# Attention inside a fused block: the transposes of the last query block move ahead of the scores of the third and fourth blocks

## The reference, cut to what matters

```python
q, k, v = (qkv[:, :, 0], qkv[:, :, 1], qkv[:, :, 2])
q = rotary_embedding(q, seq_len, HEAD_DIM)
k = rotary_embedding(k, seq_len, HEAD_DIM)
scores = jnp.einsum('bqhd,bkhd->bhqk', q, k) * scale
mask = jnp.tril(jnp.ones((seq_len, seq_len), dtype=bool))[None, None, :, :]
scores = jnp.where(mask, scores, NEG_INF)
weights = jax.nn.softmax(scores, axis=-1)
out = jnp.einsum('bhqk,bkhd->bqhd', weights, v)
out = out.reshape(batch, seq_len, NUM_HEADS * HEAD_DIM)
return jnp.einsum('bsf,fe->bse', out, W_out)
```

## Time and profile before

| | |
|---|---|
| median of 3 runs | 1304.67 us (1304.54 to 1305.31) |
| the profiled execution: its time | 1303.55 us |
| its span, first to last instruction | 1301.8 us |
| attention loop, first scores to last projection | from about 276 to about 1029 us |
| busy over the span: TensorE / VectorE / ScalarE / GpSimd | 93% / 71% / 59% / 64% |

### The profile page before, as it was taken

How to read it: one execution, slowest core, us unless ns; L and a number is a source line. 1 busy time by engine, 2 the same in 40 slices (tenths; PEclk the granted TensorE clock), 3 DMA queues, 4 the chain that set the end, 5 groups by cost and what they waited for, 6 DMA issues and landing times. The chain is left out here.

```text
span 1301.8 us, 26919 instructions
## 1 busy us (share of the span) xinstructions
PE 1209.9 (93%) x8118; PEld 894.6 (69%) x8118; DVE 929.6 (71%) x2027; ACT 764.2 (59%) x2179; POOL 827.6 (64%) x906
## 2 busy tenths in 40 slices
PE   7799999969999999999999999999999759999992
PEld 5588888846666666666666666666665658888882
DVE  6665344358888888888888888888888677633543
ACT  5655665646666656666656656656565426555552
POOL 4323356158888788787787787676666336766662
PEclk8899999989999999999999999999999959999996
DMA  9151122122221222212221222211221231113223
GB/s 306 38 205 44 49 57 69 39 67 51 60 56 37 57 58 52 52 45 52 59 54 44 51 54 50 49 39 45 50 49 34 90 114 42 47 48 111 61 64 107
DMA packets 86008, 86.44 MB, mean 66 GB/s; under 512 B 11040, under 2 KB 78496, under 8 KB 85104
## 3 DMA queue, kind: packets, MB, share of 16 engines
q1 hardware_dynamic: 74896, 65.50, 18.6%
q0 software_dynamic: 8864, 18.17, 5.2%
q10 hardware_dynamic: 2112, 1.05, 0.3%
HBM read 33.43 MB, written 17.69 MB: 39 GB/s over the span
## 5 line engine op out<-in xcount | busy, mean ns | idle before, releaser
L1605 POOL TENSOR_SCALAR at_prob<-at_prob,at_rec 128x128 f32<-128x128 f32 (+3 forms) x256 | 316.0, 1239 | 162.4 <-DVE at_rec L1787 160.9
L1888 ACT ACTIVATE at_prob<-at_s,at_nb 128x128 f32<-128x128 f32 (+3 forms) x512 | 265.4, 526 | 49.7 <-DVE at_nb L1779 45.2
L960 POOL DMA_INDIRECT f_xb<-xn_dram,f_source x142 | 141.8, 999 | 168.6 <-PE f_b L1007 104.3
L1899 ACT ACTIVATE at_probT<-at_pt 128x128 f32<-128x128 f32 (+3 forms) x256 | 105.0, 436 | 231.1 <-PE at_pt L1711 231.1
L1779 DVE TENSOR_REDUCE at_nb<-at_s 128x2 f32<-128x256 f32 (+3 forms) x256 | 208.6, 816 | 10.9 <-PE at_s L1697 10.9
L1169 DVE TENSOR_TENSOR f_hid<-f_b,f_silu 128x512 f32<-128x512 f32 x142 | 98.5, 693 | 140.5 <-PE f_b L1020 98.7
L1711 PE MATMUL at_pt<-ident,at_prob 128*128 128x128 f32 x1280 | 183.5, 275 | 1.9 <-DVE at_prob L1790 1.2
L1692 PE MATMUL at_s<-at_KT,at_QT 64*128 64x128 f32 (+3 forms) x1024 | 176.1, 463 | 6.1 <-DMA at_KT<-at_probT 4.6
L1773 DVE TENSOR_TENSOR at_turned<-at_pj,rope 128x1024 f32<-128x1024 f32 x122 | 148.8, 1220 | 40.6 <-PE at_pj L1658 40.6
L1723 PE MATMUL at_o<-at_probT,at_V 128*64 128x512 f32 (+3 forms) x1024 | 152.0, 437 | 16.1 <-DVE at_probT L1801 16.1
L1599 POOL TENSOR_TENSOR at_R<-at_turned 128x512 f32<-128x512 f32 x126 | 157.2, 1267 | 2.2 <-DMA at_KT<-at_probT 2.2
(11 more groups left out here) (298 smaller groups left out, 2141.9 us busy)
## 6 DMA issues: line engine op xcount, KB each, us to landing
at_QT<-at_R SPq DMA_DIRECT2D x128, 128.0 KB, 2.3
at_KT<-at_R SPq DMA_DIRECT2D x124, 128.0 KB, 2.3
ys_dram<-y SPq DMA_DIRECT2D x71, 64.0 KB, 1.8
xn_dram<-f_xn SPq DMA_DIRECT2D x16, 256.0 KB, 2.7
f_down<-down_t SPq DMA_DIRECT2D x2, 2048.0 KB, 8.2
f_xb<-xn_dram,f_source POOLq DMA_INDIRECT x142, 2.6
X<-x SPq DMA_DIRECT2D x4, 512.0 KB, 6.2
gate<-gate_t SPq DMA_DIRECT2D x8, 256.0 KB, 5.2
```

Source lines behind the costliest of these rows:

```text
L960: pool.indirect_dma_start(out=xb[j % AHEAD][:, :], out_offset=None, in_=xn_dram, in_offset=bass.IndirectOffsetOnAxis(ap=routing.source[:, ...
L1605: pool.tensor_scalar(w, w, rec[:, q, 1:2], None, ALU.mult).then_inc(probB_ready, 1)
L1888: act.activation(prob[q][:, h, :], s_bank[q % 2][:, h, 0:n], ACT.Exp, bias=nb[:, q, h:h + 1], scale=1.0, accum_out=sums[:, q, h:h + 1]).th ...
```

## The change

On TensorE the turns of query block 3 of step i - 1 stand before the scores of blocks 2 and 3 of step i, not behind them. On VectorE the copy of those turns stands before the maximum of block 2, not behind it. ScalarE's, GpSimd's and SyncE's lists are as they were. No instruction is added or removed.

```diff
@@ TensorE
                     if i >= 2:
                         out_project(i - 2)
+                    if last:
+                        turn_probs(i - 1, (3,))
                     if this:
                         scores(i, 2)
-                    if last:
-                        turn_probs(i - 1, (3,))
                     if i + EARLY < ROTATIONS:
                         project(i + EARLY, 0)
@@ VectorE
                     if this:
                         normalise_a(i, 0)
                         normalise_a(i, 1)
-                        maximum(i, 2)
                     if last:
                         copy_b(i - 1, 3)
                     if this:
+                        maximum(i, 2)
                         maximum(i, 3)
                     if i + EARLY < ROTATIONS:
                         rotate(i + EARLY, 0)
```

## The result

| | before | changed |
|---|---|---|
| median | 1304.99 us (4 runs, 1304.54 to 1306.97) | 1340.74 us (4 runs, 1340.1 to 1341.35) |
| ratio | | 1.0267, 95% interval 1.0254 to 1.0280 |
| span of the profiled execution | 1301.8 us | 1338.6 us |
| attention, from the first scores to the first instruction behind it | 753.6 us | 789.9 us |

The changed kernel is 35.8 us slower. 36.3 of the 36.8 us that the span grew lie in the attention (the first scores start at 276.3 before and 275.9 after, the mixture behind starts at 1029.9 and 1065.8).

A forecast was written before the change was run, and what follows sets the result against it. TensorE, busy 97.9 of 100 us, was taken as the bound, the chain through maxima and rotation to second projection ending each step; 21.6 + 2.1 + 5.7 + 1.0 = +30.4 on 1304.67 gave 1335.1 us, range 1325 to 1348.

The forecast's parts named there:

- Forecast A: Whole kernel: the moved turns wait bare for ScalarE's copy, 1335 us, own range 1328 to 1342; chance 0.84.
- The wait: TensorE, turns of block 3: ScalarE's block 2 copy ends at 4.82, turns start at 4.97 not 4.57, idling 0.40 a step.
- The chain behind it: Plain step from turns at 4.97 through scores, mask, maxima, rotation and second projection: next step at 12.10 instead of 11.63.
- the 1.40: Time from the start of VectorE's rotation to TensorE's second projection, put at 1.40 us in each step.
- The split of the 0.47: Added time per plain step: 0.40 from the turns' wait for ScalarE, 0.07 from moving the scores behind a fresh wait.
- Moments: The 7 steps with moments: 12.10 instead of 11.80, +0.30 each, 2.1 us together.
- Turns of the input: The 7 steps with turns of the input: ScalarE's copy at 5.31, step 12.59 instead of 11.77, +0.82 each, 5.7 us.
- The ends: Last steps, without projection: second scores wait for block 3's exponents, +0.5 each for two; step 1 counted as plain.
- Rival B: Turns of block 3 start at 4.57 without waiting for ScalarE: +0.07 a plain step, about +4, 1308.5 us; chance 0.05.
- D: Turns behind a wait go at the slow pace, +0.60 a step more: 1371 us, or 1353 for half; chance 0.07.
- Rival C: The wait before `weigh` goes and nothing takes its place: -13.0 us, 1292 us; chance 0.04.

The follow-up runs named there:

- the early copy: Changed kernel with ScalarE's copy of block 2 out of pt0 moved ahead of the exponents of block 1: 1340.57 us, 1.0002 of the kernel before on its chip.
- the short maximum: Block 3's maximum over its first 256 keys only: kernel before 1303.67 us (0.9988); changed kernel with ScalarE's copy moved ahead of block 1's exponents 1292.48 us (0.9909).

## Why the prediction was right

Forecast +30.4 us, measured +35.8: a sixth too little. Forecast A (a bare wait for ScalarE's copy) is what happened. By its steps:

- **The wait.** ScalarE's copy ends at 4.82 and the turns start at 4.96 (worked out 4.97). The wait as such is listed with 21.2 us in 57 times, 0.37 each. That it is the cause, the early copy shows: without it the step is 11.64.
- **The chain behind it** is named rightly, with two of its terms mis-sized that partly cancel. Turns to scores was put at 0.80, from turns that stand behind a mask; behind `out_project` and a wait it is 1.00 (636.84 - 635.84). Rotation to second projection was put at 1.40; it is 1.27 (642.14 - 640.87). Hence 12.16 and not 12.10, +0.53 a step for +0.47. Over 45 plain steps that is 2.7 us. That the sum came so near is in part luck: +0.20 and -0.13 have nothing to do with each other. The idle times it named for VectorE before the maxima (0.5) and at the second projection's weight load (0.3) came out at 0.69 and 0.39.
- **Why the 1.40 was wrong.** The prediction said that the maxima and the rotation end each step of the kernel before. They don't: the short maximum there changed no step. The 1.40 held 0.13 of slack, because the second projection started when `weigh` had got far enough, and not when the rotation was done.
- **The split of the 0.47** into 0.40 for the wait and 0.07 for the move itself is off: the move without the wait costs 0.01 (11.64 against 11.63), the wait 0.52. Turns could have started at 4.48, not at the assumed 4.57, and that makes 0.48; the turns are 0.04 slower behind it.
- **Moments:** 12.16 - 11.80 = +0.36 for +0.30. **Turns of the input:** 12.64 - 11.77 = +0.87 for +0.82, their copy at 5.31 as worked out.
- **The ends.** Steps 2 to 60 together grew by 720.9 - 688.2 = 32.7 us. Steps 61 and 62: -0.25 and +0.95 for +0.5 each, 0.70 for 1.0 together. The wait that was named is there (in step 62 the scores of block 1 wait 0.76 for the exponents of block 3), but it falls only in the second of the two, and in the first `weigh` gains. Step 1, counted as a plain one, took 13.43 against 11.78: +1.65, and why was not followed up. From step 63 to the end of the attention it is 22.6 us against 20.7, +1.9, of which the prediction had nothing: 0.9 of it falls in step 63, which waits as step 62 does, and 1.0 behind it, where the last turns of block 2 wait 1.46 for ScalarE instead of 0.42. Step 0, in which nothing is moved, took 11.3 for 11.9; kernels with the same step 0 gave 11.3 to 11.9 in other profiles.
- **Rival B** (the wait doesn't bite) and **D** (the turns run at the slow pace, 1.40) are out by the trace. D's direction was right, 0.20 of its 0.60, but hardly its reason: only 0.04 of the 0.20 goes away with the wait.
- **Rival C**, and the Trainium skill's advice that it stood for, "Perfetto Trace Analysis", section "Optimization Strategy": find the gaps of the engine in question and make what they wait for start sooner. The trace agrees with its first half, since the gap before `weigh` did close, from 13.0 us to none. The change was a loss all the same, 0.53 a step, because the instruction that was moved has a wait of its own, and the place it had been taken from was what covered it. Nor is it a gain without that wait: with the early copy the gap is closed too and the step is 11.64, because the second projection then waits for the chain through the maxima and the rotation. That place the prediction had named under rival C.

## What to carry to other kernels

An instruction that is moved forward brings its own waits with it: before moving it, list each semaphore it needs with the time at which that comes, at the new place. Here one of four came 0.34 us after the instruction ahead let go (4.82 against 4.48), and everything behind it in that engine's list was late in every turn of the loop. When several chains end within 0.2 us of each other, taking away one wait shows the next one; only a shorter piece of work (here half a maximum) showed how far down the step could go.

## What the runs showed of the hardware that was not expected

- The time from the start of one group of matmuls to the start of the next belongs to its neighbours too. The same 8 turns of block 3 take 0.80 behind a bf16 mask (to a projection), but 0.96 to scores and 0.95 to a projection behind `out_project`. `out_project` takes 1.06 to scores and 0.97 to turns. Most of this cancels when both borders are counted: the turns add 0.82 where they stood (0.23 from the mask and 0.80, less the 0.21 from mask to projection without them) and 0.87 where they went (0.97 + 0.96 - 1.06). So here a move is priced by the sum over both borders.
- With one pair of 128-column bf16 mask matmuls between the fp32 scores of two blocks and one behind them, and not both pairs behind, the same work takes 0.30 longer (2.22 against 1.92).
- The same program took 2.7% longer on one chip (1340.13 against 1305), with nearly the same granted clock in the profiles (0.964 to 0.969 there, 0.964 to 0.970 elsewhere) and the same time in the attention; nearly all of the difference lies in the mixture behind it, 304 to 308 us against 272 to 275. Why is open.
- The idle time of a weight load doesn't show that its matmul waited: 10.1 us of it stood before the second projections with the rotation 0.72 us early.
